# ScalarE's roundings of the temporal input taken in turn with the evictions of the cross queries, and that input's stores issued before the next weight loads

## The reference

```
xn = _ln(x, norm_s_w, norm_s_b)
spatial_out = _spatial_experts(xn, idx_s, sp_in_w, sp_in_b, sp_out_w, sp_out_b)
xt = _ln(x, norm_t_w, norm_t_b)
temporal_out = _temporal_experts(xt, idx_t, tq_w, tq_b, ..., tp_w, tp_b)   # returns xt + o
fused = _cross_mha(spatial_out, temporal_out, ...)    # q from spatial_out, k and v from temporal_out
x = x + fused
```

## Time and profile before

| | us |
|---|---|
| three runs | 1817.34, 1817.26, 1813.61 (median 1817.26) |
| profiled execution, its own time | 1814.99 |
| its span | 1813.0 |
| PE busy | 1651.4 (91%) |
| DVE busy | 1125.9 (62%) |
| ACT busy | 882.3 (49%) |
| POOL busy | 727.4 (40%) |
| mean granted TensorE clock | 0.962 of full |

### The profile page before, as it was taken

One profiled execution on the slowest core, in us unless ns is written; L12 is line 12 of the kernel. 1 busy time (PEld: TensorE's weight loads), 2 busy tenths in 40 slices (PEclk: granted clock), 3 DMA queues, 4 the chain that ended last, 5 costly groups with the idle time before them and its releaser, 6 DMA issues.

```text
span 1813.0 us, 27124 instructions
## 1 busy us (share of the span) xinstructions
PE 1651.4 (91%) x9904; PEld 1377.0 (76%) x9904; DVE 1125.9 (62%) x1802; ACT 882.3 (49%) x1728; POOL 727.4 (40%) x593
## 2 busy tenths in 40 slices
PE   2897989849999999987999998999999997899997
PEld 1565876538788888875878998787888886688876
DVE  7895134730488889852038887418988887853332
ACT  3894221322388788722217776207878784401100
POOL 3122020034734465032356873544544458532431
PEclk9998999969999999988999999999999998899999
DMA  3000000131212111033122230421112120011111
GB/s 106 8 24 24 0 29 12 51 143 36 57 30 57 30 30 41 12 93 141 36 57 58 58 70 7 166 63 30 29 30 57 36 81 18 20 33 41 41 40 56
DMA packets 33000, 88.40 MB, mean 49 GB/s; under 512 B 5190, under 2 KB 5660, under 8 KB 32369
## 3 DMA queue, kind: packets, MB, share of 16 engines
q1 hardware_dynamic: 32881, 86.83, 17.5%
HBM read 43.29 MB, written 12.80 MB: 31 GB/s over the span
## 4 chain that ended last, share of the span: by engine, by line
PE 75%; DVE 8%; ACT 5%; POOL 4%; DMA 3%; issue 3%; SPq 1%; DVEq 1%; POOLq 0%; ACTq 0%
PE ps L686 12%; PE ps L907 12%; PE ps L687 11%; PE ps L688 11%; PE ps L888 11%; PE ps L873 7%; PE ps L874 6%; PE ps L813 2%; DMA w_raw<-in_weights 2%; PE ps L814 1%; PE ps L923 1%; POOL F L603 1%; ACT F L1082 1%; DVE stats L1303 1%; ACT F L1175 1%
## 5 line engine op out<-in xcount | busy, mean ns | idle before, releaser
L548 POOL TENSOR_TENSOR w_hi<-w_raw,zero 128x512 fp32r<-128x512 f32 x96 | 111.7, 1163 | 712.2 <-PE ps L688 437.0
L1095 ACT ACTIVATE R<-ps 125x500 fp32r<-125x500 f32 (+3 forms) x632 | 291.2, 508 | 147.3 <-PE ps L888 145.8
L1547 DVE TENSOR_REDUCE TB<-ps 125x1 f32<-125x1250 f32 (+4 forms) x240 | 299.5, 1262 | 82.6 <-PE ps L874 56.1
L1556 DVE TENSOR_TENSOR R<-ps,R 125x500 fp32r<-125x500 f32 (+3 forms) x632 | 323.8, 568 | 10.9 <-ACT R L1095 10.9
L1082 ACT ACTIVATE F<-ps,TB 125x1250 f32<-125x1250 f32 (+4 forms) x240 | 276.0, 1157 | 88.6 <-DVE TB L1547 88.6
L907 PE MATMUL ps<-R 125*128 125x252 f32 (+1 forms) x2080 | 288.9, 286 | 2.3 <-DVE F L1599 2.3
L888 PE MATMUL ps<-ident,F 125*125 125x125 f32 x2040 | 259.3, 275 | 8.3 <-ACT F L1082 7.3
L907 PEld LDWEIGHTS ps<-R 125*128 125x128 f32 x2080 | 255.9, 189 | 2.6 <-DVE R L1556 1.6
L888 PEld LDWEIGHTS ps<-ident,F 125*125 125x125 f32 x2040 | 239.1, 189 | 11.6 <-ACT F L1082 11.3
L873 PE MATMUL ps<-R 128*125 128x512 f32 (+5 forms) x624 | 240.0, 385 | 5.1 <-DVE R L1556 3.9
L686 PE MATMUL ps<-R,w_hi 128*128 128x512 f32 (+1 forms) x576 | 209.9, 364 | 38.0 <-POOL w_lo L563 14.0
(11 more groups left out here) (175 smaller groups left out, 2459.0 us busy)
## 6 DMA issues: line engine op xcount, KB each, us to landing
R<-F SPq DMA_DIRECT2D x96, 312.5 KB, 5.2
w_raw<-in_weights SPq DMA_DIRECT2D x96, 256.0 KB, 2.6
TB<-in_x SPq DMA_DIRECT2D x10, 250.0 KB
x_d<-F SPq DMA_DIRECT2D x10, 250.0 KB
zt_d<-F SPq DMA_DIRECT2D x1, 2500.0 KB, 10.2
F<-zt_d SPq DMA_DIRECT2D x1, 2500.0 KB, 12.9
xt_d<-F SPq DMA_DIRECT2D x4, 625.0 KB, 3.6
qc_d<-F SPq DMA_DIRECT2D x4, 625.0 KB, 2.9
```

The costliest lines, as they stand in the source:

```text
L548: return eng.tensor_tensor(to, a, zero[0:to.shape[0], :].to_broadcast(list(to.shape)), ALU.add)
L1095: eng.activation(probs_run(K, n, 0, part, lo, hi), ps[0:P, 3 * (n % 2) + bank, P * (lo - j0):P * (hi - j0)] .rearrange("p (c t) -> p c t", ...
L1547: ins = eng.tensor_reduce(out=ngm[0:P, 2 * (n % 2) + part:2 * (n % 2) + part + 1], in_=flat(n % 2)[0:P, at:at + P * blocks], op=ALU.max, a ...
L1556: eng.tensor_tensor(probs_run(K, n, 1, part, lo, hi), ps[0:P, 3 * (n % 2) + bank, P * (lo - j0):P * (hi - j0)] .rearrange("p (c t) -> p c ...
```

## The change

ScalarE no longer makes all four roundings of the temporal input and then all four evictions of qc. It makes rounding 0, eviction 0, rounding 1, eviction 1, and so on. The wait for the scaled bias stands ahead of the first eviction. SyncE issues the four stores to `xt_d` before the four weight loads of qt. Nothing moves on the other engines, and no arithmetic changes.

```
@@ SyncE
             eng.dma_start(ocol[:], out_bias[ds(e_t + NEXP, 1), :, :].rearrange("a p c -> p (a c)")
                           ).then_inc(ocol_in[1], 16)
-            load_units(UNIT["qt"], 4, e_t * 16 + T0)
             for k in range(KC):
                 eng.wait_ge(sp["t"].val, k + 1)
                 eng.dma_start(xt_d[:, k, :], PB[:, k % 2, :]).then_inc((sp["t"].st0, sp["t"].st1)[k % 2], 16)
+            load_units(UNIT["qt"], 4, e_t * 16 + T0)
             for m in range(4):
                 eng.wait_ge(pj["qk"].a, 9 + m)
                 eng.dma_start(qc_d[:, m, :], QK[:, 0, m, :]).then_inc(qc_st, 16)
@@ ScalarE
             out_hi(pj["u"], 0, X1)
-            cut_hi(sp["t"], lambda k: PB[:, k % 2, :], X0, True)
-            eng.wait_ge(biasq, 2)
-            bias_cols(pj["qk"], UNIT["qc"], QK[:, 0], bcol_q, SCALE)
+            for m in range(4):
+                eng.wait_ge(sp["t"].val, m + 1)
+                eng.activation(X0[0][:, m, :], PB[:, m % 2, :], ACT.Copy).then_inc(sp["t"].hi, 1)
+                if m == 0:
+                    eng.wait_ge(biasq, 2)
+                eng.wait_ge(w_used, UNIT["qc"] + m + 1)
+                eng.activation(QK[:, 0, m, :], flat(m % 2)[:, 0:T], ACT.Identity, bias=bcol_q[:, m:m + 1],
+                               scale=SCALE).then_inc(pj["qk"].a, 1)
```

## The result

| | before | changed |
|---|---|---|
| median of the runs, us | 1815.43 (1813.07 to 1817.34, 4 runs) | 1798.56 (1797.09 to 1802.13, 4 runs) |
| profiled execution: time, span | 1814.99, 1813.0 | 1797.95, 1796.1 |
| mean granted clock | 0.962 | 0.969 |

The ratio is 0.9916 (95% interval 0.9903 to 0.9928), a clear gain of 16.9 us in the medians.

The account below looks back on a forecast made before the run. The prediction took TensorE as the bound, three quarters of the chain, stopped once at qc. Its terms 0 - 13.5 - 2.5 = -16.0 gave 1799.0 from the profiled execution, 1801.3 from the median; it said 1800, range 1795.5 to 1806.5.

Parts of the forecast that it names:

- The loop: At qc's piece 2: eviction 0 stood behind four roundings, rounding 2 behind store 0, and that behind qt's weight loads.
- Stop 13.5: TensorE's one wait at qc's piece 2 for an eviction, 13.5 us, was to go.
- clock 2.5: The piece behind TensorE's stop ran at the low clock; its 2.5 us were counted as gain.
- The 5.5 us to spare at qc's piece 2: Piece 2's region free from 819.8, piece 1 ending at 825.3, so TensorE needn't stop there.
- The sign that failed: In the trace after, GpSimd's splits were to stand 6.9 us apart through the stage.
- The store: Stores to xt_d were taken to land after the median 3.6 us, with bounds 2.9 and 5.4.
- The cover of qt's weights: qt's first weight unit was to be ready at 829.8 and wanted by TensorE at 839.2: 9.4 us.
- Rival 1: qt's weights come late behind the stores and TensorE stops at qt: gain 8.9, so 1806 us; chance 0.09.
- Rival 2: The time is given back behind the stage, or the edit misses its aim: 1815 to 1817 us; chance 0.05.
- Rival 3: Without the stop TensorE gets the low clock while working: slower, 1828 us at six low-clock pieces; chance 0.04.

Follow-up runs that it names:

- e1: Changed kernel with only ScalarE's alternation kept; SyncE again issues qt's four weight loads before the four stores to xt_d. Measured 1799.00 us, ratio 0.9907.
- e2: Changed kernel with only SyncE's reordering kept; ScalarE again makes four roundings and then four evictions. Measured 1799.43 us, ratio 0.9904.
- e3: Changed kernel with qt's four weight loads issued behind all four stores of qc. Measured 1810.36 us, ratio 0.9963.
- e4: Changed kernel with qt's four weight loads issued behind the third store of qc and ahead of the fourth. Measured 1801.93 us, ratio 0.9913.
- e5: Changed kernel; behind spatial and temporal attention each rounding waits only for its own pair's normalisation, and VectorE makes lo 0 earlier. Measured 1792.53 us, ratio 0.9873.
- e6: Kernel of e5 with GpSimd's split of the first MLP weight unit moved between roundings 6 and 7 of the MLP input. Measured 1792.25 us, ratio 0.9869.

## Why the prediction was right

- **The loop.** The forecast named one stop with two queues in it. e1 and e2 show both links: with either cut, the stop goes or shrinks to 0.7 us.
- **The size.** Stop 13.5 and clock 2.5 made 16.0; the stage lost 16.03. e3 shows the two as separate terms on a stop that was made, 7.7 and 2.4.
- **The sum against the time.** From the profiled execution it was 1799.0, measured 1797.95; 1800 was said, the median is 1798.56. The 1.0 us too little is scatter ahead of the stage. That the median came so near the 1800 is partly luck: the changed kernel's four runs spread over 5 us.
- **ScalarE and TensorE, step by step.** The times of these two engines are 1.0 us early in the changed run against those of the forecast, since the stage began 1.0 us earlier. Rounding 2 ended at 827.9 in the forecast and at 826.8 here, rounding 3 at 834.9 and 833.7. The 5.5 us to spare at qc's piece 2 were there (eviction 0 ended at 818.8, piece 1 at about 824.3).
- **The sign that failed.** GpSimd's splits don't stand 6.9 us apart, as the forecast said that they would. The first of qt's units starts at 826.48, 15.9 us after the split before it (810.57), and the next two follow as their loads land:

```profile
829.95 1.03 POOL L548 TENSOR_TENSOR w_hi<-w_raw,zero 128x512 fp32r<-128x512 f32 x1
832.62 1.04 POOL L548 TENSOR_TENSOR w_hi<-w_raw,zero 128x512 fp32r<-128x512 f32 x1 [0.26 <-DMA w_raw<-in_weights]
```

  The forecast's own times spoke against this sign: with the first load at 824.7 the splits can't keep step with TensorE's pieces. They measure the pieces only where GpSimd waits for TensorE, and the evictions had to be used instead.
- **The store.** The 3.6 us to landing came from a stretch in which the first store was issued 0.4 us behind a weight load and took 4.34. The four stores now took 2.9 to 3.7, median 3.1.
- **The cover of qt's weights.** This term was off by 1.2 us. It was to be 9.4 us; the first unit was ready at 829.99 and wanted at 838.2, so 8.2. The load, issued at 823.0 just behind store 3, took 3.5 us until GpSimd started, not 2.6, and the split 3.5, not 2.4 (below). The 2.6 is the median of all weight loads; in e3 and e4, too, the first load stands 0.5 us behind a store, and it took 3.4 and 3.7. The forecast also said that a load announced only behind store 3 changes no term. In its own times store 3 lands at 827.9 and the load at 827.3, so 0.6 us of the cover hung on it, though nothing of the sum. e4 shows how much of the cover was real: loads issued about 10 us later cost 1.4.
- **The rivals.** Rival 1 didn't happen, and e3 shows what it would have looked like. Rival 2: from the second eviction of qt to VectorE's first TENSOR_REDUCE of the temporal attention it is 71.65 us before and 71.66 after (869.09 to 940.74, 852.04 to 923.70), so nothing was given back there. That everything behind the stage agrees too, 943.9 and 944.1, is partly chance: in e1 to e4 it lies between 942.3 and 946.8, but a loss of 16 us can't hide in that. Rival 3: TensorE was busy from 811 to 900 without the stop, and the clock is 1.00.

## What to carry to other kernels

When TensorE stops for long at one place, follow the chain until it comes back to TensorE. This loop through queues was cut at either of two places, by moving instructions that stood in front of others without being needed by them, and the second cut added only margin. Ask of each wait whether it is wider than what it guards; the same question gave another 7.6 us in e5 (7.0 at the two places themselves). Count the clock with a long stop (2.4 and 2.5 us here, for stops of 7.7 and 13.5), not with one as short as those of e2 and e4, and read a gain below the scatter of the runs from one stage, between two instructions that every kernel has.

## What the runs showed of the hardware

VectorE and GpSimd held each other up. In the changed kernel VectorE's `lo` 2 and GpSimd's split of qt's first unit fell together:

```profile
826.79 2.04 DVE L1368 TENSOR_TENSOR R<-F,R 128x1250 fp32r<-128x1250 f32 x1 [4.36 <-ACT R L1235]
```

```profile
826.48 1.04 POOL L548 TENSOR_TENSOR w_hi<-w_raw,zero 128x512 fp32r<-128x512 f32 x1 [13.49 <-DMA w_raw<-in_weights]
827.60 2.39 POOL L563 TENSOR_TENSOR w_lo<-w_raw,w_hi 128x512 fp32r<-128x512 f32 x1
```

Alone they take 1.46 and 1.29 us. GpSimd's first operation ends at 827.52, and 1.31 later VectorE's ends at 828.83; GpSimd's second ends at 829.99, 1.16 after that. So each ran, nearly at its own length, when the other had finished. This agrees with the Trainium skill, "SBUF — State Buffer", section "Terms": the two engines take a shared pair of ports in turn, each for a whole instruction, and the other waits. The forecast hadn't counted this; it took 1.1 us of a cover of 9.4.

It happened again with `lo` 3 (833.73 to 835.19, its usual 1.46), and there GpSimd alone was held, until 1.15 us behind VectorE's end:

```profile
833.74 2.60 POOL L563 TENSOR_TENSOR w_lo<-w_raw,w_hi 128x512 fp32r<-128x512 f32 x1
```

The rows of before had it as well: GpSimd's operation at 818.53 took 1.98 us instead of 1.04 beside VectorE's `lo` at 818.15. In e6 the same two engines cost the gain that was expected.
